# A selective scan in steps of 1024 columns, two batches at a time, with one exponential for two steps

## The reference

```python
A = -exp(A_log)                                  # 256 channels x 16 states
h = exp(dt_t * A) * h + dt_t * B_t * x_t         # for t = 0..511, h starts at 0 in each batch
y_t = sum over the 16 states of h * C_t
return y + D * x
```

## Time and profile before

| | |
|---|---|
| time, three runs | 722.69, 724.18, 725.13 us; median 724.18 |
| span of the profiled execution | 713.3 us; the median of the runs is 10.9 us above it |
| first scan, from its first recurrence to the end of the last | 57.55 to 218.54 us: 161.0 us |
| second scan | 309.24 to 471.01 us: 161.8 us |
| busy in the span | PE 90%, DVE 76%, ACT 74%, POOL 62% |

### The profile page before, as it was taken

The page is one execution under the profiler, slowest core; times in us unless marked ns, Lnnn a source line. Parts: engine busy times, 40 slices in busy tenths (PEclk is TensorE's granted clock), DMA queues, the critical chain, the costliest instruction groups (busy, mean ns, idle before and its releaser), DMA issues.

```text
span 713.3 us, 13062 instructions
## 1 busy us (share of the span) xinstructions
PE 640.6 (90%) x4408; PEld 550.0 (77%) x4409; DVE 542.7 (76%) x1030; ACT 526.5 (74%) x1295; POOL 443.4 (62%) x396
## 2 busy tenths in 40 slices
PE   4758999999994759489999999989999999999995
PEld 2348999999994423389999999988677777777684
DVE  6897999999998795969999999996932644434316
ACT  2959999999996969699999999975543562222224
POOL 0036999999998250359999999991575134333400
PEclk9959999999997869679999999999999999999998
DMA  6032555544450000134535454544123233333173
GB/s 185 7 72 80 147 143 141 145 141 143 141 149 1 0 0 6 26 98 147 159 130 155 135 149 142 147 141 151 59 97 110 74 104 105 108 105 106 55 244 118
DMA packets 57579, 77.86 MB, mean 109 GB/s; under 512 B 8112, under 2 KB 38480, under 8 KB 57520
## 3 DMA queue, kind: packets, MB, share of 16 engines
q1 hardware_dynamic: 53728, 66.75, 32.0%
q0 software_dynamic: 3792, 10.36, 4.1%
HBM read 58.21 MB, written 18.87 MB: 108 GB/s over the span
## 4 chain that ended last, share of the span: by engine, by line
PE 77%; DVE 10%; ACT 10%; issue 1%; POOL 1%; DMA 1%; ACTq 0%; DVEq 0%
PE bank L1153 25%; PE bank L1176 15%; PE bank L1221 12%; PE bank L1155 4%; ACT tok_a L771 3%; PE bank L1229 3%; PE bank L1230 3%; PE bank L1172 2%; PE bank L1066 2%; DVE st L373 2%; DVE arena L471 1%; PE bank L1323 1%; PE bank L1297 1%; PE bank L1289 1%; PE bank L1092 1%
## 5 line engine op out<-in xcount | busy, mean ns | idle before, releaser
L976 POOL TENSOR_TENSOR arena<-arena,rings 128x512 f32<-128x512 f32 x256 | 317.6, 1284 | 21.6 <-DVE arena L574 20.5
L574 DVE TENSOR_TENSOR_SCAN arena<-rings,bank 128x512 f32<-128x512 f32 x256 | 300.1, 1208 | 15.1 <-PE bank L1155 7.5
L1153 PE MATMUL bank<-rings,tok_a 128*128 128x128 f32 x1536 | 216.9, 278 | 4.7 <-ACT rings L868 4.7
L1153 PEld LDWEIGHTS bank<-rings,tok_a 128*128 128x128 f32 x1536 | 195.4, 195 | 5.3 <-issue 5.3
L878 ACT ACTIVATE rings<-arena,a_sb 128x512 f32<-128x512 f32 x256 | 170.1, 715 | 0.4 <-DVE arena L574 0.4
L1176 PE MATMUL bank<-ident,arena 128*128 128x128 f32 x1024 | 152.4, 273 | 1.1 <-POOL arena L976 1.1
L868 ACT ACTIVATE rings<-ident,b_tok 128x128 f32<-128x128 f32 x384 | 125.3, 393 | 0.4 <-ACT tok_a L833 0.4
L1176 PEld LDWEIGHTS bank<-ident,arena 128*128 128x128 f32 x1024 | 119.4, 141 | 1.9 <-POOL arena L976 1.8
L1016 POOL DMA_INDIRECT y_tok<-rings,dest x47 | 44.9, 955 | 85.1 <-DVE rings L715 84.8
L1155 PE MATMUL bank<-ident,rings 128*128 128x128 f32 x256 | 70.7, 276 | 0.0
L950 ACT ACTIVATE silu<-bank 128x176 f32<-128x176 f32 x47 | 14.9, 317 | 73.4 <-PE bank L1221 73.4
(11 more groups left out here) (179 smaller groups left out, 942.0 us busy)
## 6 DMA issues: line engine op xcount, KB each, us to landing
rings<-c_rows SPq DMA_DIRECT2D x128, 256.0 KB, 3.4
w_sb<-w SPq DMA_DIRECT2D x18, 352.0 KB, 4.3
x_sorted<-zeros SPq DMA_DIRECT2D x47, 128.0 KB, 3.4
rings<-x_sorted SPq DMA_DIRECT2D x47, 128.0 KB, 2.0
arena<-w SPq DMA_DIRECT2D x2, 2048.0 KB, 12.7
residual<-x SPq DMA_DIRECT2D x4, 512.0 KB, 5.8
tok_a<-y_tok SPq DMA_DIRECT2D x4, 512.0 KB, 7.5
w_sb<-y_tok SPq DMA_DIRECT2D x4, 512.0 KB, 8.4
```

The source lines that it names most:

```text
L574: dve.tensor_tensor_scan(state[:, u % STATE_RING, :], abar[:, u % ABAR_RING, :], bank[u % B_RING][:, :], 0.0, ALU.mult, ALU.add).then_inc( ...
L976: pool.tensor_tensor(s, s, crep[:, k % CREP_RING, :], ALU.mult).then_inc(hc_ready, 1)
L1153: pe.matmul(o, tok_a[:, c, h * P:(h + 1) * P], v_ring[:, s % V_RING, j, 0:P], start=True, stop=True)
```

## The change

- A step is now one piece of 1024 columns for both halves: one recurrence, one product by C (C is read twice through a broadcast), one semaphore count. The rings keep their bytes: four states of 1024 columns, two PSUM inputs of two banks each. SUM_LAG is 3 steps instead of 6 units.
- The order of steps is new (`batch_state`): batches 0 and 1 alternate step by step through 32 steps (PAIR), then batches 2 and 3.
- So an exponential takes one channel half of two neighbouring batches, 1024 columns, and two of them serve two steps (`decays`). The buffers of a pair of steps are two in all: one pair is written, one is read. A pair's exponentials wait for the recurrence of the last step that used the buffer, three steps back.
- ACT's loop is now: the exponentials of steps s and s + 1, then the input of s, then the input of s + 1. The exponentials of steps 0 and 1 stand before the last copies of u.
- `inputs` uses the diagonal for two chunks of four, in every third step for three (`diagonals`); the other chunks are written out as products and transposed.
- The two halves of a 1024-column recurrence must not run into each other: after u is computed, dt of the second half's first column is set to 1e30, so that its decay is 0 (POOL, `edge_ready`); A is kept at or below -1e-25.
- The last step runs in halves, for recurrence, product and total.
- y of batches 0 and 1 is copied after steps 33 and 34, its statistics are taken in the even steps 36 to 54. y of batches 2 and 3 is read from PSUM after the scan, and `first_y` is reordered for it.
- The clearing of gatedT moves from the start of the kernel to after the second scan, as its memory now holds decays.

```diff
-STATE_RING, ABAR_RING, CREP_RING, V_RING, B_RING = 8, 4, 4, 4, 4
+STATE_RING, ABAR_RING, CREP_RING, V_RING, B_RING = 4, 4, 4, 4, 2
+PAIR = 2 * N
+LEAST_RATE, LONG_STEP = 1e-25, 1e30
-SUM_LAG = 6
-DIAGONAL = 3
+SUM_LAG = 3
...
-        first_y = [("y_stat", 0), ("y_stat", 1), ("y_stat", 2), ("y_add", 0), ("y_add", 1), ("y_stat", 3), ("y_add", 2)]
+        first_y = [("y_stat", 0), ("y_stat", 1), ("y_add", 0), ("y_add", 1), ("y_stat", 2), ("y_stat", 3), ("y_add", 2)]
...
+                    dve.wait_ge(b_ready, base + s + 1)
+                    dve.wait_ge(abar_ready, H * ((base + s) // 2 + 1))
+                    if s >= STATE_RING:
+                        dve.wait_ge(state_free, base + s + 1 - STATE_RING)
+                    h_s, decay_s = state[:, s % STATE_RING, :], abar_pair[s // 2 % 2][:, s % 2]
+                    if s < STEPS - 1:
+                        dve.tensor_tensor_scan(h_s, decay_s.rearrange("p h t -> p (h t)"), both[s % B_RING][:, :],
+                                               0.0, ALU.mult, ALU.add).then_inc(h_ready, 1)
...
+                    if s in (PAIR + 1, PAIR + 2):
+                        y_out(l, s - PAIR - 1)
+                    elif PAIR + 4 <= s < PAIR + 4 + 2 * (2 * CQ + 2) and s % 2 == 0:
+                        y_stat_part(l, *divmod((s - PAIR - 4) // 2, CQ + 1))
...
+                    if q == Q - 1:
+                        decays(l, 0)
...
+            def decays(l, s):
+                b, n = batch_state(s)
+                if n == 0:
+                    act.wait_ge(a_ready, l + 1)
+                    act.wait_ge(dt_ready, (l * BATCH + b + 2) * H)
+                    act.wait_ge(edge_ready, l * BATCH + b + 2)
+                if s >= ABAR_RING:
+                    act.wait_ge(h_ready, l * STEPS + s + 2 - ABAR_RING)
+                for h in range(H):
+                    act.activation(abar_pair[s // 2 % 2][:, :, h, :],
+                                   dtT[:, h, b * SEQ:(b + 2) * SEQ].rearrange("p (r t) -> p r t", r=2), ACT.Exp,
+                                   scale=a_sb[l][:, h, n:n + 1]).then_inc(abar_ready, 1)
...
                 for s in range(AHEAD):
                     input_part(s)
-                for s in range(STEPS):
-                    decay(s)
-                    if s + AHEAD < STEPS:
-                        input_part(s + AHEAD)
+                for s in range(AHEAD, STEPS, 2):
+                    decays(l, s)
+                    input_part(s)
+                    input_part(s + 1)
...
+                def inputs(s):
+                    pe.wait_ge(v_ready, base + s + 1)
+                    if s >= B_RING:
+                        pe.wait_ge(h_ready, base + s + 1 - B_RING)
...
+def batch_state(s):
+    return s // PAIR * 2 + s % 2, s % PAIR // 2
...
+def diagonals(s):
+    return 3 if s % 3 == 2 else 2
```

More of the change, by code:

```diff
@@ L166, in sandwich_kernel @@
         w_buf = early[:, 2 * C * D:3 * C * D].rearrange("p (h t) -> p h t", h=H)
-        bank = [ctx.enter_context(nc.psum_tensor(f"bank{i}", [P, 512], F32)) for i in range(8)]
+        both = [ctx.enter_context(nc.psum_tensor(f"both{i}", [P, H * SEQ], F32)) for i in range(B_RING)]
+        bank = [both[i // H][:, i % H * SEQ:(i % H + 1) * SEQ] for i in range(H * B_RING)]
+        bank += [ctx.enter_context(nc.psum_tensor(f"bank{i}", [P, 512], F32)) for i in range(H * B_RING, 8)]
         ysum = bank[4:6]
@@ L1001, in _ @@
                 stage(name, q, 2)
+            pool.wait_ge(h_ready, 2 * STEPS)
+            pool.memset(gatedT[:, :, :, :], 0.0).then_inc(gT_cleared, 1)
             pool.wait_ge(sorted_zeroed, 16 * TILES)
@@ L1118, in stage @@
                         pe.wait_ge(scaled, q * H)
+                    else:
+                        pe.wait_ge(y_normed, (Q - 1) * CQ)
                     pe.wait_ge(ftr_copied, (q + 1) * H)
@@ L1138, in scan @@
             def scan(l):
[L1140 to L1155 removed]
+                base = l * STEPS
+                def inputs(s):
+                    pe.wait_ge(v_ready, base + s + 1)
+                    if s >= B_RING:
+                        pe.wait_ge(h_ready, base + s + 1 - B_RING)
+                    for h in range(H):
+                        for j in range(CQ):
+                            o = both[s % B_RING][:, h * SEQ + j * P:h * SEQ + (j + 1) * P]
+                            if j < diagonals(s):
+                                c = batch_state(s)[0] * CQ + j
+                                pe.matmul(o, tok_a[:, c, h * P:(h + 1) * P], v_ring[:, s % V_RING, j, 0:P], start=True, stop=True)
+                            else:
+                                ins = pe.transpose(o, v_ring[:, s % V_RING, j, h * P:(h + 1) * P], ident[:, :])
                     ins.then_inc(b_ready, 1)
@@ L1183, in scan @@
                 pe.wait_ge(utr_copied, (l + 1) * Q * 2)
-                for u in range(BATCH * UNITS):
-                    inputs(u)
-                    if u >= SUM_LAG:
-                        total(u - SUM_LAG)
-                for u in range(BATCH * UNITS - SUM_LAG, BATCH * UNITS):
-                    total(u)
+                for s in range(STEPS):
+                    inputs(s)
+                    if s >= SUM_LAG:
+                        total(s - SUM_LAG)
+                for s in range(STEPS - SUM_LAG, STEPS):
+                    total(s)
             def weight_turns():
```

147 lines of the change are left out of this document (66 added, 81 removed).

## The result

| | before | after |
|---|---|---|
| runs beside each other, median | 724.65 us (722.69 to 727.37, 4 runs) | 732.41 us (731.62 to 734.24, 4 runs) |
| ratio after / before | | 1.0114 [1.0083, 1.0145] |
| span of the profiled execution | 713.3 us | 729.8 us |
| first scan, first recurrence to the end of the last | 57.55 to 218.54: 161.0 | 59.82 to 224.11: 164.3 |
| second scan | 309.24 to 471.01: 161.8 | 316.10 to 480.37: 164.3 |

The change costs 7.8 us, not the 16.5 by which the spans differ. A second profile of the kernel before (the first experiment) has the first one's scans within 0.4 us, but a span of 723.6. The 10 us lie in the experts at the end, and they are no part of the change. Three of the experiments had single executions far longer than the others of their kernel; medians and ratios here leave these out.

The account below looks back on a forecast made before the run. The prediction took a closed waiting chain through DVE, ACT and PE to bound the scan. First scan 5.8 plus second 4.4 gave +10.2 on a 713.3 span, 723.5; with 10.9 for the median, 734.4 us, range 728 to 741.

Parts of the forecast that it names:

- The chain: In the scan: recurrences, ACT's exponentials and input, PE's input, next recurrence wait in a circle; 2.465 us a step.
- The round: Four steps of the scan, once around the chain: 9.86 us; sixteen make 157.8 us.
- D * x: PE matmuls at steps 0, 1, 32 and 33, 3.55 us in each place; 5.7 us a scan beyond spare time.
- the copies and statistics: Copies of y after steps 33 and 34, statistics in even steps: 0 to 3.0 us a scan, 0.5 taken.
- The start: Beginning of each scan: first recurrence later, at 59.7 instead of 57.55 in the first; +2.1 and +1.5 us.
- POOL's later end: End of each scan: POOL finishes 2.7 us after the last recurrence instead of 2.04, delaying the tail's first shift; +0.6.
- batch 2's root: Each tail: the root comes behind ACT's eight normalisations, its reciprocal and shift behind it; +0.6 us, bounds 0 and 1.8.
- The 10.9 us above the span: Whole kernel: the runs' median lies 10.9 us above the profiled span, added to 723.5 to give 734.4.
- A: Rival, faster: the chain does not close, the longest list sets the pace; scans of 154.5, 716.4 us; chance 0.12.
- B: Rival, no change: the chain stands with pieces at their low end, a round of 9.6, edges half; near 723; chance 0.08.
- C: Rival, much slower: the long exponential keeps its fixed part twice, 1.23 us; 6 a scan, 746; chance 0.05.
- D: Rival: PE waits more and its clock drops to 1.2 GHz in the scan; 31 us more; chance 0.03.

Follow-up runs that it names:

- the first experiment: The kernel before once more, with no edit, for a second profile of it; 726.82 against 726.13 us, ratio 1.0003.
- the inputs ahead: The kernel after with ACT's list reordered only: four inputs of B before the loop, later inputs a pair ahead of their exponentials; 715.36 us, ratio 0.9852.
- the run at 705.25 us: From the set with the inputs ahead and four-instruction shifts in the tails and f_norm's batch 0; runs cluster at 705 to 706, 710 and 715 us, ratio 0.9915.

## Why the prediction was right, and which terms were not

**Direction, size and mechanism: right.** 10.2 us were forecast, 7.8 came (ratio 1.0114). The chain is shown by its waits, by taking it out of the kernel after (0.9852) and by putting it into the kernel before (1.0586). One sign did not come as written: ACT was to wait some 0.3 before each pair's exponentials. In steps 8 to 32 it waited 0.07 to 0.30 before those that go to `rings` and mostly not at all before those that go to `late` (0.13 at most). Its own list, 4 x 2.39 = 9.56 us, is only 0.2 to 0.4 shorter than a round, so the chain and ACT's list lie close together.

**The pieces.** Forecast and measured: exponential 1.04 and 1.045 (121.04 to 123.13, two); recurrence 2.28 and 2.28 (2283 ns in the page's group), from start to start 2.19 and 2.20; product on POOL 2.34 and 2.33 (a pair of 4.70 less one of 2.37); hop to ACT 0.02 and 0.03. The groups of the recurrence and the exponential in the page of after (busy, mean ns | idle before):

```profile
L579 DVE TENSOR_TENSOR_SCAN arena<-rings,both 128x1024 f32<-128x1024 f32 x64 | 144.8, 2283 | 30.1 <-PE both L1182 29.5
...
L877 ACT ACTIVATE rings<-arena,a_sb 128x1024 f32<-128x1024 f32 x64 | 70.1, 1143 | 15.2 <-DVE arena L579 14.2
```

Three widths of rows 2 and a straight line through them gave a width that no row showed.

**The round.** From step 8 to step 32, in which nothing but the loop runs, the kernel after takes 59.49 us (81.95 to 141.44 in the timeline of DVE), 9.92 a round; 9.86 was forecast.

```profile
59.82 4.46 DVE L579 TENSOR_TENSOR_SCAN arena<-rings,both 128x1024 f32<-128x1024 f32 x2 [4.05 <-PE both L1182]
...
81.95 4.49 DVE L579 TENSOR_TENSOR_SCAN arena<-rings,both 128x1024 f32<-128x1024 f32 x2 [1.01 <-PE both L1182]
...
141.44 4.49 DVE L579 TENSOR_TENSOR_SCAN arena<-rings,both 128x1024 f32<-128x1024 f32 x2 [0.74 <-PE both L1182]
...
204.58 4.49 DVE L579 TENSOR_TENSOR_SCAN arena<-rings,both 128x1024 f32<-128x1024 f32 x2 [0.45 <-PE both L1182]
```

These are steps 0, 8, 32 and 56. Four of the six rounds between 8 and 32 take 9.78 or 9.79, and every third one 10.13 or 10.22; the places of the third diagonal repeat with the same period, 12 steps. The chain therefore makes 16 x 9.92 = 158.7 of the scan, where 157.8 was written. That is less than the 161.0 of the kernel before: as predicted, the rounds alone do not make the change slower. The loss is what comes on top, 5.6 us; before, 64 x 2.51 = 160.6 left 0.4 for it.

**The step that was mis-sized: what comes on top of the chain.** For D * x 5.7 was forecast, 2.8 and 3.1 were measured. It lies in two places of equal work, yet cost 2.0 at the first and 1.0 at the second, where the copies of y (1.2 us each) hold DVE back in the same round. For the copies and statistics 0.5 was taken from a range of 0 to 3.0, on the ground that D * x covers them. Without D * x, steps 32 to 56 still take 62.11, where six rounds are 59.5: 2.6. So it was near the far end of that range. That the copies hid a part of D * x, and not D * x the copies, is how I read it; no run leaves out the copies. The two errors, 2.7 too much and 2.1 too little, nearly cancel; with the round's 0.06 the scan came to 164.3 against 163.5. That the total was near is in part luck: these errors cancelled, and 2.4 us of tails (below) were forecast that did not come.

**The start: right in place, open as a term.** The first recurrence was forecast for 59.7 and came at 59.82; the second scan's input stage is 1.3 longer (83.1 instead of 81.8 from f_norm's first ACT to the first recurrence), 1.5 was forecast. But starting the first scan 1.6 earlier brought nothing (ratios 1.0133 and 1.0114): ACT had the same pieces to do, only in another order, and recurrence 1 came 0.3 later. How much of the 1.9 and 1.3 a start that is truly earlier would give back, no run shows. A moment at which a stage starts is not a cost until it is shown that its end moves with it.

**The tails: wrong.** 0.6 for POOL's later end and 0.6 for batch 2's root, in each, 2.4 in all; nothing of it came. From the last recurrence to f_norm's first ACT it is 8.9 us after and 9.0 before, and in the second tail 23.2 and 23.3 to the first expert's matmul. POOL did end later as written: its last half from 225.55 to 226.83, 2.72 after the recurrences. But the first shift did not wait for that. The timeline of DVE and POOL in the kernel after:

```profile
224.21 0.17 DVE L393 SCALAR_TENSOR_TENSOR shift<-mom,rstd 128x4 f32<-128x4 f32 x1
...
224.32 1.27 POOL L988 TENSOR_TENSOR arena<-arena,rings 128x512 f32<-128x512 f32 x1
...
224.49 1.11 DVE L393 SCALAR_TENSOR_TENSOR shift<-mom,rstd 128x4 f32<-128x4 f32 x1
...
225.55 1.28 POOL L991 TENSOR_TENSOR arena<-arena,rings 128x512 f32<-128x512 f32 x1
```

The first shift got in at the change of POOL's instructions, as POOL's last long product ended at 224.36, and took 0.17; the second waited one product, 1.11. Before, it was the first that waited, 1.95. The Trainium skill (SBUF — State Buffer, "Who interferes with whom") says that a VectorE instruction with two SBUF inputs contends with a GpSimd instruction that reads SBUF, and that the port pair they share is an exclusive lock. The traces agree: 1.11 us beside a product of 1.27, and none for the four instructions with one SBUF tensor as input that took its place. The length of a wait does not follow from one instruction: with the inputs ahead the shift waited 2.80 us, through four additions of 0.69, to the end of the run. What was wrong was to charge the wait through POOL's last instruction: here it ended where POOL changed from one product to the next, there where the run of additions ended.

**The sum, place by place**, against the second profile of before: start 1.9 (2.1 forecast), first scan 3.3 (2.5), first tail 0 (1.2), the stage up to the second scan 1.3 (1.5), second scan 2.4 (1.7), second tail 0 (1.2); together 8.9 (8.7 read at the first expert's matmul), forecast 10.2. The runs give 7.8 with an interval of 6.0 to 10.5.

**The 10.9 us above the span.** I took the distance between the median and the span of before as something that stays. In every run of which both are known it is 1.8 to 1.9 us (725.41 and 723.6; 731.62 and 729.8). The profiled execution of before was a short one: 713.3, where the timed runs less this distance are 721 to 725.5. The method held, as the sum was added to the median, but what I called a distance was a difference between executions.

**The rivals.** A (the longest list sets the pace, 716.4) is near what the kernel does with the inputs ahead: 715.36, with scans of 153.2 where 154.5 was reckoned and a longer first tail. As a forecast for this kernel it is refuted. B needed a round of 9.6. C needed an exponential of 1.23 and is refuted by the 1.045; what it would have cost was 746, and the run that builds it took 746.65. D is refuted by the clock, 0.99 over rows 1's stretch.

## What to carry to other kernels

When work is put into one in-order queue behind a wait on a ring, follow that wait through everything behind it to the engine that releases it: if it comes back to itself, add up the round, since a round can be longer than every engine's list. Moving the inputs one pair ahead, a change of order alone, turned +1.1% into -1.5%. Before removing a wait, look at which instruction is next to need the same thing: it may take the wait over, as the shifts did.

## What the runs showed of the hardware that was not expected

- The kernel before took 725 to 727 us in most sets of runs and 716.49 (715.29 to 717.54) in one, and its two profiles are 713.3 and 723.6 long. The difference of the two profiles lies in the experts, 219.0 and 228.8 us from the first expert's matmul to the end (219.0 also in the profile of the run at 705.25 us): idle time at L619 without a releaser that the profile shows, 11.0 us in seven pieces of up to 3.1 in the second profile, in the kernel after 12.9 with one of 5.5. The clock has a part in it: in the second profile PE stands still from 540 to 542 us, at a granted clock of 0.93 in that stretch and 1.00 ahead of it, and then runs at 0.50 from 542 to 548; in the first it is busy for all of 530 to 550 at 1.00. PE idled before the clock fell, so the clock is not the start of it; what is stays open. It is larger than the change, and only runs beside each other gave the sign of the change.
- A VectorE instruction of 0.17 us lasted 2.80, to the end of a run of eight GpSimd additions back to back, and 0.17 when it came at the change between two products.
- Four one-column instructions in its place took 0.58 beside the same additions, and did not wait.
